# Target scores of a graph attention: taken from a column of the message product and spread over the partitions by a DRAM write and read

## The reference

```python
att = jax.nn.sigmoid(xs @ W_att[:d] + xd @ W_att[d:] + b_att)   # xs = x[src], xd = x[dst]
messages = (xs @ W_msg + b_msg) * att
aggregated = jax.ops.segment_sum(messages, dst, num_segments=num_nodes)
```

## Time and profile before

| | |
|---|---|
| median of 3 runs | 4071.94 us (4071.8 to 4072.37) |
| the profiled execution's own time | 4071.28 us |
| its span in the trace | 4069.2 us |
| TensorE busy | 3723.1 us |
| VectorE busy | 3125.1 us |
| ScalarE busy | 2450.5 us |
| GpSimd busy | 1342.8 us |
| steps 392 and on (attention) | 1374.2 to 1952.0 us |
| score products (line 2307) | 1199.2 to 1516.6 us |

### The profile page before, as it was taken

How to read it: one execution, slowest core, us unless ns; L and a number is a source line. 1 busy time by engine, 2 the same in 40 slices (tenths; PEclk the granted TensorE clock), 3 DMA queues, 4 the chain that set the end, 5 groups by cost and what they waited for, 6 DMA issues and landing times.

```text
span 4069.2 us, 59937 instructions
## 1 busy us (share of the span) xinstructions
PE 3723.1 (91%) x17037; PEld 2913.9 (72%) x17037; DVE 3125.1 (77%) x5676; ACT 2450.5 (60%) x4604; POOL 1342.8 (33%) x1941
## 2 busy tenths in 40 slices
PE   0118889999999999999899999999999999999999
PEld 0116678888888644555688888888888888888887
DVE  9989956677687778887668767877876876786685
ACT  1119966656656787787565555555555555566655
POOL 0021135534545310000362343244244234446624
PEclk9999999999999999999899999999999999999999
DMA  2019964545543322221144454444444444434444
GB/s 64 0 45 367 365 218 136 158 137 144 156 128 108 93 70 75 71 66 55 52 115 119 117 142 130 120 136 133 121 132 138 119 118 140 122 98 111 117 133 136
DMA packets 320608, 509.09 MB, mean 125 GB/s; under 512 B 118979, under 2 KB 187324, under 8 KB 319895
## 3 DMA queue, kind: packets, MB, share of 16 engines
q1 hardware_dynamic: 299484, 452.24, 38.7%
q0 software_dynamic: 7856, 46.93, 3.2%
q10 hardware_dynamic: 12938, 6.05, 0.7%
HBM read 396.99 MB, written 43.87 MB: 108 GB/s over the span
## 4 chain that ended last, share of the span: by engine, by line
PE 50%; issue 0%; ACT 0%; DVE 0%; POOL 0%; ACTq 0%; POOLq 0%
PE ps L2224 41%; PE ps L2340 3%; PE ps L2341 3%; PE ps L2342 1%; PE ps L2343 1%; PE ps L2370 0%; PE ps L2256 0%; PE ps L2326 0%; PE ps L2365 0%; PE ps L2262 0%; PE ps L2247 0%; ACT wide L2063 0%; PE ps L2239 0%; PE ps L2381 0%; PE ps L2191 0%
## 5 line engine op out<-in xcount | busy, mean ns | idle before, releaser
L2224 PE MATMUL ps<-wide,hi 128*128 128x512 f32 (+2 forms) x5537 | 2148.9, 390 | 19.8 <-issue 9.5
L2224 PE MATMUL ps<-wide,lo 128*128 128x512 f32 (+2 forms) x5537 | 2076.5, 379 | 0.0
L2063 DVE CAST wide<-ring 128x1536 fp32r<-128x1536 uint8 (+2 forms) x1274 | 1311.5, 1029 | 492.5 <-PE ps L2224 486.9
L2224 PEld LDWEIGHTS ps<-wide,hi 128*128 128x128 f32 x5537 | 1041.8, 188 | 224.5 <-issue 29.8
L2224 PEld LDWEIGHTS ps<-wide,lo 128*128 128x128 f32 x5537 | 1043.6, 188 | 188.7
L2063 ACT CAST wide<-ring 128x768 fp32r<-128x768 uint8 (+1 forms) x1274 | 1152.8, 905 | 3.7 <-DMA ring<-count 2.9
L2433 ACT CAST hi<-high 128x128 fp32r<-128x128 f32 x1274 | 380.7, 299 | 1038.2 <-PE ps L2224 623.4
L2162 POOL TENSOR_TENSOR lo<-hN,high 128x128 fp32r<-128x128 f32 x686 | 561.5, 822 | 750.5 <-PE ps L2224 437.7
L2162 POOL TENSOR_TENSOR lo<-hB,high 128x128 fp32r<-128x128 f32 x588 | 494.1, 841 | 752.6 <-PE ps L2224 495.3
L2220 PE MATMUL ps<-hN,hB 128*128 128x512 f32 (+1 forms) x1274 | 525.3, 569 | 5.6 <-DVE aggT L2396 4.2
L2426 ACT ACTIVATE hN<-aggT,source_scores 128x512 f32<-128x512 f32 (+1 forms) x637 | 428.9, 695 | 118.0 <-PE ps L2220 86.9
(11 more groups left out here) (246 smaller groups left out, 3403.2 us busy)
## 6 DMA issues: line engine op xcount, KB each, us to landing
ring<-count SPq DMA_DIRECT2D x490, 320.0 KB, 3.0
ring<-count SPq DMA_DIRECT2D x441, 256.0 KB, 2.7
ring<-count SPq DMA_DIRECT2D x490, 224.0 KB, 2.6
wide<-aggT POOLq DMA_DIRECT2D x49, 896.0 KB, 6.2
count<-aggT SPq DMA_DIRECT2D x49, 800.0 KB, 4.0
hB<-mid SPq DMA_DIRECT2D x192, 32.0 KB, 1.9
hN<-mid SPq DMA_DIRECT2D x192, 32.0 KB, 1.9
hB<-squares SPq DMA_DIRECT2D x96, 32.0 KB, 2.1
```

The costliest lines, as they stand in the source:

```text
L2063: return copy(wide[:, g % WIDE_SLOTS, c0:c1].rearrange("p (t u f) -> p t u f", u=2, f=P), rows[:, g % row_slots, c0:c1].rearrange("p (t f ...
L2224: ins = e.matmul(ps[:, c, 0:size], part[:, g % CUT_SLOTS, :], wide[:, g % WIDE_SLOTS, w0:w0 + size], start=k == 0 and part is hi, stop=k = ...
```

## The change

The target vector `W_att[d:]` becomes a further column of `w_msg`, so the message product has 130 columns and yields messages, source scores and target scores, the latter with nodes on partitions. The product with `att_rep`, its copy on ScalarE and the waits that they needed are gone. Instead:

- VectorE copies the column to SBUF at `sent`, between the two instructions that were there;
- SyncE writes it to DRAM (`written`), 256 single words, so that the nodes of a chunk lie in a row there;
- SyncE reads that row back into all 128 partitions of `aggT` (`scored`). It waits for the write first.

SyncE's loop is ahead by the nine slots of the ring. `g - row_slots - LEAVE[...]` puts the write into SyncE's turn 29 steps after the chunk's start and the read into turn 31, behind the row load of that turn. Each row load there waits until the other engines have widened (or, in the attention, weighed) the step nine before.

```diff
 STORE_AT = 15
-LEAVE = {"first": 0, "relu": 3, "second": 4, "shift": 7, "seen": 7, "root": 8, "even": 11, "turned": 12, "state": 15, "message": 16, "score": 17,
-         "sent": 19, "scored": 20}
+LEAVE = {"first": 0, "relu": 3, "second": 4, "shift": 7, "seen": 7, "root": 8, "even": 11, "turned": 12, "state": 15, "message": 16, "sent": 19,
+         "written": 20, "scored": 22}
 ENTER = {"normal": 0, "turned": 0, "added": 2, "root": 3, "even": 5, "back": 5, "plain": 7, "coded": 7, "code": 9, "encoded": 10, "entered": 12, "source": 12}
...
     message: tuple
-    target: object
     target_scores: object
...
             bn = self.enter.bn if self.enter is not None else layers[-1].bn if attends else None
+            if leaving:
+                flat_scores = nc.dram_tensor(f"flat_scores_{nc.next_id()}", [NP], F32, kind="Internal").ap()
             if final is not None or leaving:
...
             rows = ring[:, 0:row_slots * ROW_BYTES].rearrange("p (j f) -> p j f", f=ROW_BYTES)
+            if leaving:
+                columns = ring[:, row_slots * ROW_BYTES:row_slots * ROW_BYTES + 4 * NB].bitcast(F32)
             if self.enter is not None:
...
                                 .then_inc(s[f"moved{u}"], 16)
+                    for c in self.due(g - row_slots - LEAVE["written"], "leave"):
+                        e.wait_ge(s["lv_sent"], c.late)
+                        with nc.allow_non_contiguous_dma(reason="a score of each node, nodes on partitions"):
+                            e.dma_start(flat_scores[c.cols].rearrange("(k p) -> p k", p=P), columns[:, c.first:c.first + c.blocks])\
+                                .then_inc(s["lv_written"], 16)
+                    for c in self.due(g - row_slots - LEAVE["scored"], "leave"):
+                        e.wait_ge(s["lv_written"], 16 * c.late)
+                        e.dma_start(layers[c.layer].target_scores[:, c.cols],
+                                    flat_scores[c.cols].rearrange("(a f) -> a f", a=1).to_broadcast([P, c.size])).then_inc(s["lv_scored"], 16)
                     if final is not None and n + 1 == len(layers) and k == STORE_AT and q == 2:
...
                                 e.wait_ge(s["lv_relu"], len(leaves))
-                                e.wait_ge(s["lv_scored"], len(leaves))
                             if self.enter is not None and g == 0:
...
                             e.wait_ge(s["lv_relu"], c.late - 1)
-                        scored = self.leaves_before(c.at - LEAVE["score"])
-                        if scored:
-                            e.wait_ge(s["lv_scored"], scored)
                         e.matmul(ps[:, 4, 0:c.size], layers[c.layer].first[0], net.aggT[:, c.cols], start=True, stop=True)\
...
                         for b in range(c.blocks):
-                            ins = e.matmul(ps[:, 7, b * (D + 1):(b + 1) * (D + 1)], net.hT[:, (c.first + b) * P:(c.first + b + 1) * P],
+                            ins = e.matmul(ps[:, 7, b * (D + 2):(b + 1) * (D + 2)], net.hT[:, (c.first + b) * P:(c.first + b + 1) * P],
                                            layers[c.layer].message[0], start=True, stop=True)
                         ins.then_inc(s["lv_message"], 1)
-                    for c in self.due(g - LEAVE["score"], "leave"):
-                        e.wait_ge(s["lv_state"], c.late)
-                        e.wait_ge(s["lv_relu"], self.leaves_before(g + 1))
-                        if c.late > 1:
-                            e.wait_ge(s["lv_scored"], c.late - 1)
-                        e.matmul(ps[:, 4, 0:c.size], layers[c.layer].target, net.hT[:, c.cols], start=True, stop=True)\
-                            .then_inc(s["lv_score"], 1)
-
                     for c in self.starting[g]:
...
                         if k == 0:
-                            e.wait_ge(s["lv_scored"], max(d.late for d in leaves if self.part_of(d.third) == q))
+                            e.wait_ge(s["lv_scored"], 16 * max(d.late for d in leaves if self.part_of(d.third) == q))
                         for c, (w0, size) in enumerate(SUMS[q]):
...
                         e.copy(net.hT[:, c.cols], ps[:, 6, 0:c.size]).then_inc(s["lv_state"], 1)
-                    for c in self.due(g - LEAVE["scored"], "leave"):
-                        e.wait_ge(s["lv_score"], c.late)
-                        e.copy(layers[c.layer].target_scores[:, c.cols], ps[:, 4, 0:c.size]).then_inc(s["lv_scored"], 1)
                     for c in self.due(g - CHAIN["relu"], "decode"):
...
                     for c in self.due(g - LEAVE["sent"], "leave"):
-                        made = ps[:, 7, 0:c.blocks * (D + 1)].rearrange("p (b f) -> p b f", f=D + 1)
+                        made = ps[:, 7, 0:c.blocks * (D + 2)].rearrange("p (b f) -> p b f", f=D + 2)
                         _, row, column = layers[c.layer].message
...
                                         made[:, :, D:D + 1], column, None, ALU.add).then_inc(ch.sem, ch.up())
+                        e.tensor_copy(columns[:, c.first:c.first + c.blocks].rearrange("p (b a) -> p b a", a=1), made[:, :, D + 1:D + 2])\
+                            .then_inc(ch.sem, ch.up())
                         e.tensor_tensor(layers[c.layer].messages[:, c.cols].rearrange("p (b f) -> p b f", f=P), made[:, :, 0:D],
...
         b_msg = sb("b_msg", [P, D])
-        w_msg = sb("w_msg", [P, D + 1])
+        w_msg = sb("w_msg", [P, D + 2])
         att_rep = sb("att_rep", [P, P])
...
                    (b3[:, :], column(a["L3_gnn_b"])),
-                   (w_msg[:, D:D + 1], a["L1_gnn_W_att"][0:D, :]),
+                   (w_msg[:, D:D + 1], a["L1_gnn_W_att"][0:D, :]), (w_msg[:, D + 1:D + 2], a["L1_gnn_W_att"][D:2 * D, :]),
                    (w_att[:, :], a["L1_gnn_W_att"].rearrange("(g p) o -> p (g o)", p=P)),
...
             with nc.sbuf_tensor(f"msg_{nc.next_id()}", [P, NP], F32) as msg:
-                net.messages(msg, w_msg[:, :], b_msg[:, :], b_att[:, 0:1], source_scores)
+                net.messages(msg, w_msg[:, 0:D + 1], b_msg[:, :], b_att[:, 0:1], source_scores)
                 net.target_scores(att_rep[:, :], scores)
...
             leave = Leave(layer_scales(layers0 - 1)[0], (w12[:, layers0 - 1, 1, :], last_shift[:, :]), (w_msg[:, :], b_msg[:, :], b_att[:, 0:1]),
-                          att_rep[:, :], scores, source_scores, messages)
+                          scores, source_scores, messages)
             Flow(net, [layer_scales(n) for n in range(layers0 - 1)] + [leave, Attend(gated, scores, source_scores, states_bn[:, :])],
```

## The result

The change makes the kernel slower. Before, 4072.15 us (median of 4 runs, 4071.8 to 4074.86); with the change, 4117.32 (4 runs, 4115.36 to 4119.35). The ratio is 1.0109, 95% interval 1.0096 to 1.0121: 45 us lost where 12 were forecast to be won. The profiled execution of the change took 4116.7 us, span 4114.3.

A forecast was written before the change was run, and what follows sets the result against it. TensorE, busy for 91% of the span, was taken to bound the kernel. Gains of 3.2 + 6.3 + 3.0 less 0.3 made 12.2 us off, so 4059.7 us, with an 8-in-10 range of 4055.5 to 4067.5.

The forecast's parts named there:

- Stretch C: First third of the attention stretch, from 1376 us: seven score products gone at 0.43 us each, 3.0 us gained.
- A and B: Steps 294 to 342 (A) and 343 to 391 (B): 3.2 and 6.3 us gained, 0.3 charged for VectorE's copies.
- GpSimd's chain: In steps 343 to 391, eight small GpSimd instructions per chunk could swallow three of ten scores; those taken as 0.4 us.
- Past the attention: From the attention's end on: all at the old distances, 12 us earlier.
- the ReLU's wait: In steps 343 to 391, the score product waited once for a chunk's ReLU; its removal gives 1.3 us.
- the other wait, for ScalarE's copy: First dense product no longer waits for ScalarE's copy of an older score; two TensorE idles, 1.6 us in all.
- the landing of the write: SyncE's write of 256 single words to DRAM: taken to land in 3 us, between rows at 2.6 and 14.7.
- signs of being wrong: Periods of 9.1 or more, steps starting at low parts' end, a late attention table load, or writes landing in over 5 us.
- The price of a packet: DMA engines, 35 ns a packet: 256 packets cost 0.6 us of all 16, nothing on the path.
- the entry: ScalarE's start of the attention, waiting for the eighteenth score: read there 1.9 us early; under 1 us if it took 6.
- The slower rival: Write lands late, SyncE blocks, row loads' ring runs dry: at 10 us landing 24 us slower, 4096; chance 0.05.
- the deciding point: Landing time of the write, about 9 us, from which the dry ring decides over the gain.

The follow-up runs named there:

- Experiment 3: The change, with the column transposed on VectorE and written as eight runs of 128 bytes in four transfers, write still waited for; 4060.21 us, ratio to before 0.9972.
- experiment 7: Experiment 3 with the 25 score products put back on TensorE, into a bank that nobody reads; 4071.12 us, ratio to before 0.9992.
- experiment 1: The change with its writes still issued but not waited for, each read taking its words from another DRAM array; 4065.44 us, ratio to before 0.9981.
- Experiment 2: The change with the 25 writes left out, and the reads taken from another array without a wait; 4061.34 us, ratio to before 0.9972.
- experiment 8: The change with the read four steps behind the write instead of two, and four semaphores in turn; 4087.85 us, ratio to before 1.0031.

## Why the prediction was wrong

**The gain was right.** Experiment 3 is the change with a landing as short as I assumed: 4060.2 us, where I forecast 4059.7. By its trace, from the first step at 543.5 to the end are 3515.4 us; before, 3527.4. That is 12.0 of the 12.2 us of the sum, closer than its terms deserve, since two misses offset. The terms:

- *Stretch C, 3.0:* from the first to the last attention product 577.8 us before, 574.8 here. Exact.
- *A and B, 3.2 + 6.3 - 0.3 = 9.2:* the first attention product comes 832.4 us after the first step before, 822.2 here: 10.2, 1.0 more than forecast. The first dense product of step 344 parts it, at 729.3 before and 726.0 here: 3.3 in A (2.9 forecast, with the 0.3 charged there) and 6.9 in B (6.3). In A the starts of two first dense products were to be 8.9 apart:

```profile
L2281 PE MATMUL ps<-aggT,w x2: 377/380/382, 1232.9 to 1233.1; 128*128 128x256 f32 x2
...
L2281 PE MATMUL ps<-aggT,w x2: 377/380/382, 1241.7 to 1241.9; 128*128 128x256 f32 x2
```

They are 8.8, and VectorE's idles on TensorE in these periods are gone, with a copy and a transposition in them. It did not take over, and with 6.9 of at most 7.2 in B little was swallowed behind GpSimd's chain.
- *Past the attention, nothing:* it is 1.2 us longer than before. It lies behind TensorE's last product, and it is hardly chance: from there to the end are 7.8 us before and 8.0 in experiment 7, and 8.7 to 9.7 in all twelve traces of kernels without the score products. The sum has no term for it, and what sets it stays open.
- *Products against waits:* experiment 7 puts the products and the ReLU's wait at 10.0 by the traces (10.5 forecast). I had the other wait, for ScalarE's copy, at 1.6; by the traces experiment 7 is 2.0 faster than before from the first step on. The times say 0.08% (interval 0.17% less to 0.01% more), which holds 1.6 us and can't confirm it.

**The step that failed is the landing of the write:** "I take 3, as quiet stretches are the nearer". It was 9.7. I named two rows as its bounds, one load of 768 words at 2.6 and one of 384 at 14.7, and took the nearer by traffic. Both rows read single words from DRAM. The write puts single words into DRAM, the other direction, and neither row shows that. With 256 words apart, 3 would have done (2.5). Side by side it did not. The nearness that counted was layout in DRAM, not traffic. A landing of over 5 us was also one of the prediction's own signs of being wrong.

**The price of a packet failed with it.** I took 35 ns from the earlier trace rows, 0.6 us of all engines for 256 packets. Side by side a word keeps an engine busy for some 0.20 us more than apart, so 256 of them are 3.3 us of all 16. "On the path they are nothing" was off by 4.1 us, not through the ring but through reads that land late: ScalarE waited 4.4 at the entry in experiment 1.

**The slower rival was the right one, at a chance of 0.05, and its lateness came out to the microsecond, in part by luck.** It had 36 us late at a landing of 10. ScalarE's last cast before the attention begins at 1392.39, 849.5 after the first step; in experiment 3 at 1356.94, 813.4: 36.1 late. But writes are 11.3 apart in the ten chunks and 10.5 in the eight, where the rival had 10.3 in both, some 11 us more in all; and between the two groups, which it left out, SyncE wins lead back:

```profile
1315.16 9.80 SPq L2103 DMA_DIRECT2D ring<-count  x11
```

Eleven row loads go out in 9.8 us, where eleven steps take 17.8 (at 1.62). The two errors offset.

The rival also left out the entry. There I wrote "Cost nothing; if the read took 6, still under 1 us", which assumed that SyncE is on time. After ScalarE's last cast the eighteenth read waits for the rest of the seventeenth write's landing (to 1397.87) and the whole of its own write's (to 1408.42), and lands 5.4 later: 20.7 us. 36.1 and 20.7 are 56.8; the first attention product comes 878.8 - 822.2 = 56.6 later than in experiment 3. Less the gain of 12, that is the 45 lost, where the rival said 24 (4096 us). A wait that is late on one queue has to be followed to every instruction that the queue feeds, with the lateness in it.

**The Trainium skill's warning** ("DMA: Bandwidth & Descriptors", Rules for kernel authors), that a strided last dimension is lowered to one descriptor per element and should be made contiguous, was the evidence against the change, and I gave it the weight of the 35 ns. Experiment 2's packet count agrees with it (256 packets a write), and experiment 3 is its remedy. The Trainium skill ("DMA: Bandwidth & Descriptors", Specifications) says that below 512 bytes the DMA engines read, modify and write. Taken to make every small piece slow, that would hold for 128 pieces of 64 bytes (2.4 us) and 256 of 4 bytes apart (2.5) too; here they are not slow, and the runs decide.

**The chances.** 0.75 for faster leaned on an assumed 3 us between ends of 2.6 and 14.7, with the deciding point at 9. A quantity that no row shows, with bounds on both sides of its deciding point, deserved more than 1 in 20 for the far side.

## What to carry to other kernels

Before a small write to DRAM is waited for on a queue that also streams, ask what the instructions behind it can bear, and price the landing by a row of the same layout in DRAM; if there is none, treat it as unknown. A column that lies across partitions is best turned on chip first (0.21 us on VectorE) and written in runs: here that turned 45 us of loss into 12 of gain. And a queue that is late runs its steps at issue speed, so a distance counted in steps between a transfer and its wait (3.2 us planned here, 0.9 found) vanishes just when it is needed.

## What the runs showed of the hardware

- 256 words of 4 bytes, each from its own partition, land in 2.5 us in SBUF, in 2.5 in DRAM at 64 bytes apart, in 3.4 at 16 bytes apart, and in 9.7 side by side. 16 words side by side take 2.8, 128 take 8.6, and 128 pieces of 64 bytes 2.4.
- Such writes slow others down: while they were under way unwaited (experiment 1), row loads of 224 KB landed in 9.2 us instead of the 2.5 of experiment 2, and reads of 128 KB in 9.0 instead of 3.3. Overlapping, they slow each other: in stretch B, from the second of the eight on, a write took 9.1 to 10.8 us alone (the change), 10.6 to 12.7 in experiment 1 and 12.3 to 14.5 in experiment 8.
- What the engines or the memory do with neighbouring words was not looked into. The runs show that the cost follows adjacency in DRAM, and that it bends with the number: 0.3 us over the landing of words apart at 16, 6.1 at 128 and 7.2 at 256.
